# Adaptive-norm block with linear attention and a routed expert stage: padding rows written block by block during the attention stage, a later turn of the weight maxima, filling matmuls, one turning transfer per tile

## What is computed

```python
def reference(x, qkv_w, qkv_b, out_w, out_b, W_in, in_norm_w, Wr, expert_bias, Wg, Wu, Wd, enorm_w,
              out_norm_w, W_out, c, wmod):            # x: 16 x 256 x 128
    sa, ca, ga, sb, cb, gb = split(silu(c) @ wmod, 6)  # one row per batch; |ga|, |gb| at least 0.25
    h = layernorm(x) * (1 + ca) + sa
    x = x + ga * attention(h)
    h = layernorm(x) * (1 + cb) + sb
    return x + gb * experts(h)

def attention(h):                                      # 16 heads of 8
    q, k, v = heads(h @ qkv_w.T + qkv_b)
    q, k = relu(q) + 1e-6, relu(k) + 1e-6
    kv = cumsum(einsum('bhld,bhle->bhlde', k, v), axis=2)
    num = einsum('bhld,bhlde->bhle', q, kv)
    den = maximum(einsum('bhld,bhld->bhl', q, cumsum(k, axis=2)), 1e-6)
    return (num / den) @ out_w.T + out_b

def experts(s):                                        # 4096 tokens, 8 experts, 2 of them per token
    h = rmsnorm(s @ W_in.T) * in_norm_w
    logits = h @ Wr.T
    idx = top_k(logits + expert_bias, 2)
    gates = softmax(logits[idx])
    out = sum(gates[e] * rmsnorm((silu(h @ Wg[e].T) * (h @ Wu[e].T)) @ Wd[e].T) * enorm_w[e] for e in idx)
    return (rmsnorm(out) * out_norm_w) @ W_out.T
```

## Time and profile before

| | |
|---|---|
| median of 3 runs | 413.69 us (413.61 to 415.18) |
| the profiled execution | 414.08 us |
| its span | 412.2 us |
| mean granted TensorE clock | 0.939 |
| busy: TensorE, VectorE, ScalarE, GpSimd | 354.4, 323.8, 291.9, 236.5 us |

### The profile page before, as it was taken

One profiled execution on the slowest core, in us unless ns is written; L12 is line 12 of the kernel. 1 busy time (PEld: TensorE's weight loads), 2 busy tenths in 40 slices (PEclk: granted clock), 3 DMA queues, 4 the chain that ended last, 5 costly groups with the idle time before them and its releaser, 6 DMA issues.

```text
span 412.2 us, 12923 instructions
## 1 busy us (share of the span) xinstructions
PE 354.4 (86%) x3757; PEld 307.9 (75%) x3758; DVE 323.8 (79%) x1037; ACT 291.9 (71%) x814; POOL 236.5 (57%) x211
## 2 busy tenths in 40 slices
PE   7899998999999999982069999999999999990464
PEld 4788886888888888861049889989899898980443
DVE  5568998899999999976928887878778877870696
ACT  5465776888888888546328878778778787773595
POOL 0665585688888888856341645454454445453441
PEclk9999998999999999995559999999999999997698
DMA  7899000000000000111423333333333333213833
GB/s 217 356 368 363 2 28 26 8 30 27 26 26 26 26 26 26 34 40 51 131 40 54 68 71 70 62 71 60 64 64 71 60 69 65 57 34 110 351 94 94
DMA packets 46563, 35.68 MB, mean 87 GB/s; under 512 B 36291, under 2 KB 42070, under 8 KB 45750
## 3 DMA queue, kind: packets, MB, share of 16 engines
q1 hardware_dynamic: 41862, 25.40, 21.9%
q0 software_dynamic: 4544, 9.39, 7.0%
q10 hardware_dynamic: 128, 0.53, 0.5%
HBM read 18.69 MB, written 13.47 MB: 78 GB/s over the span
## 4 chain that ended last, share of the span: by engine, by line
PE 70%; DVE 10%; ACT 6%; issue 5%; DMA 4%; POOL 1%; SPq 1%; DVEq 0%; ACTq 0%; POOLq 0%
PE bank L1474 12%; PE bank L1723 9%; PE bank L1724 8%; PE bank L1725 8%; PE bank L1738 4%; PE bank L1740 4%; PE bank L1554 4%; PE bank L1739 4%; PE bank L1497 3%; DVE prod L960 2%; ACT junk L835 2%; DVE wmaxs L1056 1%; PE bank L1561 1%; DMA cst<-consts 1%; PE bank L1581 1%
## 5 line engine op out<-in xcount | busy, mean ns | idle before, releaser
L559 POOL DMA_INDIRECT expert_rows<-late,to_place x78 | 79.2, 1015 | 85.9 <-DVE late L1333 73.3
L1723 PE MATMUL bank<-late,w_hi 128*128 128x256 f16 x312 | 86.4, 277 | 15.1 <-DMA late<-dispatched 13.7
L1724 PE MATMUL bank<-late,w_hi 128*128 128x256 f16 x312 | 86.4, 277 | 0.0
L1725 PE MATMUL bank<-late,w_lo 128*128 128x256 f16 x312 | 86.3, 276 | 0.0
L518 POOL TENSOR_TENSOR kv<-kv,v 128x1024 f32<-128x1024 f32 x32 | 67.7, 2134 | 32.0 <-ACT kv L686 32.0
L1319 DVE SCALAR_TENSOR_TENSOR kv<-bank,uscale,kv 128x512 f32<-128x512 f32 x78 | 58.5, 750 | 30.4 <-ACT kv L777 18.6
L536 POOL DMA_INDIRECT dispatched<-rows,pos x64 | 67.3, 1051 | 25.7 <-issue 18.2
L1474 PE MATMUL bank<-cst,kv 128*128 128x128 f32 x576 | 74.3, 279 | 0.0
L777 ACT ACTIVATE kv<-bank,descale 128x512 f32<-128x512 f32 x78 | 53.6, 687 | 24.0 <-PE bank L1725 20.1
L1474 PEld LDWEIGHTS bank<-cst,kv 128*128 128x128 f32 x576 | 68.9, 193 | 0.3 <-issue 0.2
L783 ACT ACTIVATE kv<-kv 128x512 f16<-128x512 f32 x78 | 48.8, 625 | 16.8 <-DVE kv L1319 12.3
(11 more groups left out here) (233 smaller groups left out, 733.2 us busy)
## 6 DMA issues: line engine op xcount, KB each, us to landing
late<-wguT SPq DMA_DIRECT2D x1, 4096.0 KB, 17.8
late<-expert_rows SPq DMA_DIRECT2D x1, 2064.0 KB, 10.9
gates_bc<-gate_rows SPq DMA_DIRECT2D x1, 2048.0 KB, 6.9
wd<-wdT SPq DMA_DIRECT2D x1, 2048.0 KB, 25.0
out<-kv SPq DMA_DIRECT2D x16, 128.0 KB, 1.8
late<-dispatched SPq DMA_TRANSPOSE x78
expert_rows<-late,to_place POOLq DMA_INDIRECT x78
late<-expert_rows SPq DMA_DIRECT2D x1, 1032.0 KB, 6.5
```

The source lines that it names most:

```text
L559: pool.indirect_dma_start(ybuf, bass.IndirectOffsetOnAxis(ap=to_place[:, s, r:r + 1], axis=0), yt[:, s, r, :], None).then_inc(y_scat[s], 16)
L1723: mm(o, w_hi[:, w], hi, start=True, stop=False)
L1724: mm(o, w_hi[:, w], lo, start=False, stop=False)
L1725: last = mm(o, w_lo[:, w], hi, start=False, stop=True)
```

## The change

Seven edits:
1. `tail_f`, `tail`, `tail_done` and the eight late transfers go. In their place SP writes padding to all rows of all regions: block s (rows 256 s to 256 s + 255 of all eight regions, 17 blocks) goes out when the KV projection of batch s+2 is done and block s-2 has landed. `positions` of batch b waits for block b, so that real rows are written over padding. SP waits for the blocks and the scatters only after it has the table and its registers.
2. TensorE's turn of the weight maxima goes from the first half of step 7 to the second, `weight_power` behind the second products, the spreading matmul to the end of the step and into another bank, and `weight_scale` behind `positions` and `count_chosen`.
3. `norm_shift` computes both halves in one instruction.
4. `keep_busy`, matmuls of 512 columns whose results nobody reads, stands at six places: 5, 13, 3, 12, 24 and 8 of them. Ahead of the last 8, TensorE waits for the scatters.
5. One turning transfer of 256 columns per tile takes the place of two of 128.
6. The weight columns are addressed by bytes (`columns_of`).
7. ScalarE makes its four parts of `wd_hi` in a row, without the transfers between them.

```diff
+            regions = hbuf[0:E * REGION, :].rearrange("(e s p j) w -> s p e (j w)", e=E, p=16, j=R // 16)
+            padding = filler[0:E * R, :].rearrange("(e p j) w -> p e (j w)", p=16, j=R // 16)
+            for s in range(REGION // R):
+                sp.wait_ge(kv_ps, min(s + 3, B))
+                if s >= 2:
+                    sp.wait_ge(padded[s % 2], 16 * (s // 2))
+                sp.dma_start(regions[s], padding).then_inc(padded[s % 2], 16)
-            sp.wait_ge(tail_done, 1)
-            tail_regs = [sp.alloc_register(f"tail{e}") for e in range(E // 2)]
-            sp.load(tail_regs, tail[0:1, 0:E // 2])
-            for e in range(E // 2):
-                row = sp.snap(tail_regs[e], min_val=0, max_val=E * REGION - R)
-                sp.dma_start(hbuf[bass.ds(row, R), :].rearrange("(p j) w -> p (j w)", p=16),
-                             filler[e * R:(e + 1) * R, :].rearrange("(p j) w -> p (j w)", p=16)).then_inc(filled, 16)
-            sp.wait_ge(scattered[0], 16 * NT * K * (B // 2))
-            sp.wait_ge(scattered[1], 16 * NT * K * (B // 2))
-            sp.wait_ge(filled, 16 * (E + 1))
             sp.wait_ge(table_done, 1)
...
-                for half in range(2):
-                    sp.dma_start(hT3[:, s, half], hbuf16[bass.ds(row, R), half * D:(half + 1) * D],
-                                 transpose=True).then_inc(slot_ld[s], 16)
+                sp.dma_start(hT3[:, s], hbuf16[bass.ds(row, R), 0:2 * D], transpose=True).then_inc(slot_ld[s], 16)
...
                 sp.load(row_regs, tile_row[0:1, bass.ds(TURN * i, TURN)])
+                if not again_turn(i):
+                    sp.wait_ge(filled, 16)
+                    for s in range(2):
+                                sp.wait_ge(padded[s], 16 * ((REGION // R + 1 - s) // 2))
+                    sp.wait_ge(scattered[0], 16 * NT * K * (B // 2))
+                    sp.wait_ge(scattered[1], 16 * NT * K * (B // 2))
...
@@ norm_shift
-                for t in range(NT):
-                    last = nc.vector.tensor_scalar(nmr_[:, p, t:t + 1], mv_[:, p, t, 0:1], -1.0, rs_[:, p, t:t + 1],
-                                                   ALU.mult, ALU.mult)
-                last.then_inc(nm_done, 1)
+                nc.vector.scalar_tensor_tensor(nmr_[:, p, :], mv_[:, p, :, 0], -1.0, rs_[:, p, :], ALU.mult,
+                                               ALU.mult).then_inc(nm_done, 1)
@@ positions
                 dve.wait_ge(ohs_done, b + 1)
+                dve.wait_ge(padded[p], 16 * n)
@@ VectorE's step
                     running_products(att, 0)
-                    if scale:
-                        weight_power(att)
...
                 if att is not None:
+                    running_products(att, 1)
                     if scale:
-                        weight_scale(att)
-                    running_products(att, 1)
+                        weight_power(att)
...
                     positions(rb, rp, rn)
                     count_chosen(rb, rp)
+                if scale:
+                    weight_scale()
@@ running_state
-                    if scale and cc == 1:
-                        if t == 0:
-                            pe.wait_ge(wmax_done, 1)
-                            mm(MAX_ROW, wmax[:], ident, start=True, stop=True)
-                        else:
-                            pe.wait_ge(wpow_done, 1)
-                            mm(MAX_ALL, ones[0:1, :], wpow_row[:], start=True, stop=True)
+                    if scale and t and cc == 1:
+                        pe.wait_ge(wmax_done, 1)
+                        mm(MAX_ROW, wmax[:], ident, start=True, stop=True)
@@ TensorE's step
                     head_sums(att, 0)
                     head_sums(att, 1)
+                if scale:
+
+                    pe.wait_ge(wpow_done, 1)
+                    pe.wait_ge(ohs_done, rte[0] + 1)
+                    mm(MAX_ALL, ones[0:1, :], wpow_row[:], start=True, stop=True).then_inc(wall_ps, 1)
+
+            def keep_busy(bank, n):
+                for _ in range(n):
+                    mm(bank[:].rearrange("p (a n) -> p a n", n=P), ones16[:],
+                       ones16[:].unsqueeze(1).to_broadcast([P, 4, P]), start=True, stop=True)
@@ TensorE's drain
                 head_sums(b15, 1)
+                pe.wait_ge(cum_used[1][1], B)
+                keep_busy(CUM[1], 5)
                 spread(*b15)
                 ranks(*b13)
                 turn(*b14)
                 project(*b15)
                 into_experts(*b14)
+                keep_busy(CUM[1], 13)
                 ranks(*b14)
                 turn(*b15)
+                keep_busy(CUM[1], 3)
                 into_experts(*b15)
+                keep_busy(CUM[1], 12)
                 ranks(*b15)
...
             mm(TOTAL, ones16[:], oh_all[:, B, NT * K, :], start=True, stop=True).then_inc(total_ps, 1)
+            keep_busy(CUM[0], 24)
...
+            def columns_of(w, e, per_expert, at):
+
+                return w.bitcast(U8)[:, bass.ds(e * (2 * per_expert) + 2 * at, 2 * P)].bitcast(F16)
...
-                    w = bass.ds(e * F + (part * E * F + (h * (FC // 2) + c) * P), P)
+                    wh, wl = (columns_of(w[:], e, F, part * E * F + (h * (FC // 2) + c) * P) for w in (w_hi, w_lo))
...
             pe.wait_ge(moe_ld, 32)
+            pe.wait_ge(scattered[0], 16 * NT * K * (B // 2))
+            pe.wait_ge(scattered[1], 16 * NT * K * (B // 2))
+            keep_busy(CUM[0], 8)
             turn_of_tiles(0, first=True)
```

More of the change, by code:

```diff
@@ L21 @@
 U32 = mybir.dt.uint32
+U8 = mybir.dt.uint8
 ALU = mybir.AluOpType
@@ L315, in block_kernel @@
         ln_st, ln2_st = two("ln_st"), sem("ln2_st")
+        padded = two("padded")
         scattered, yb_ld, stored = two("scattered"), [sem(f"yb_ld{i}") for i in range(4)], four("stored")
@@ L320, in block_kernel @@
             sem(n) for n in ("count_done", "rank_ps", "ohs_done", "pos_done"))
-        ph2, total_ps, tail_done, table_done, wmaxs_done, wmax_done, wscale_done, whi_done, wlo_done = (
-            sem(n) for n in ("ph2", "total_ps", "tail_done", "table_done", "wmaxs_done", "wmax_done",
+        ph2, total_ps, table_done, wmaxs_done, wmax_done, wscale_done, whi_done, wlo_done = (
+            sem(n) for n in ("ph2", "total_ps", "table_done", "wmaxs_done", "wmax_done",
                              "wscale_done", "whi_done", "wlo_done"))
-        wpow_done = sem("wpow_done")
+        wpow_done, wall_ps = sem("wpow_done"), sem("wall_ps")
         gate_diff, gate_sig = sem("gate_diff"), sem("gate_sig")
@@ L342, in block_kernel @@
         MAX_ROW = CUM[1][0:1, THIRD * P:THIRD * P + P]
-        MAX_ALL = CUM[1][:, THIRD * P:THIRD * P + 1]
+        MAX_ALL = FFN[:, L + NT * E:L + NT * E + 1]
         SQUARE_STEPS = range(B - WN - DN // 2, B - WN)
@@ L755, in _ @@
             pipelined(act, step, drain)
[L757 to L769, removed]
+            for c in range(DN):
                 projection_high(c)
@@ L1072, in weight_power @@
             def weight_power(att):
-                dve.wait_ge(cum_ps[0][1], att[0] + 1)
+                dve.wait_ge(cum_ps[1][1], att[0] + 1)
                 then(nc.vector.tensor_reduce(wmax_row[:], MAX_ROW, AX.X, ALU.max))
@@ L1078, in weight_power, with weight_scale @@
                                         ALU.bitwise_and).then_inc(wpow_done, 1)
-            def weight_scale(att):
-                dve.wait_ge(cum_ps[1][1], att[0] + 1)
+            def weight_scale():
+                dve.wait_ge(wall_ps, 1)
                 then(nc.vector.tensor_copy(wpow[:], MAX_ALL))
@@ L1218, in second_shift @@
             def second_shift(b, p, n):
-                dve.wait_ge(ln2_rs, b + 1)
-                nc.vector.scalar_tensor_tensor(nmr2[:, p, :], mv2[:, p, :, 0], -1.0, rs2[:, p, :], ALU.mult,
-                                               ALU.mult).then_inc(ln2_nm, 1)
+                norm_shift(b, mv2, rs2, nmr2, ln2_rs, ln2_nm, p)
             def drain(b12, b13, b14, b15):
@@ L1262, in _ @@
             then(nc.vector.tensor_copy(total[:], TOTAL))
-            then(nc.vector.tensor_tensor(tail_f[:], total[0:1, :], cst[0:1, C_REG:C_REG + E], ALU.add))
-            nc.vector.tensor_copy(tail[:], tail_f[:]).then_inc(tail_done, 1)
             nj = TOK // R
@@ L1710, in experts @@
                 return [pe.snap(r, min_val=0, max_val=E - 1) for r in ex_regs]
+            def columns_of(w, e, per_expert, at):
+                return w.bitcast(U8)[:, bass.ds(e * (2 * per_expert) + 2 * at, 2 * P)].bitcast(F16)
             def gate_up(t, s, i, e, h, part):
                 if h == 0 and part == 0:
-                    pe.wait_ge(slot_ld[s], 32 * (i + 1))
+                    pe.wait_ge(slot_ld[s], 16 * (i + 1))
                 hi, lo = hT3[:, s, 0], hT3[:, s, 1]
@@ L1720, in gate_up @@
                     o = (G, U)[part][h][:, c * R:(c + 1) * R]
-                    w = bass.ds(e * F + (part * E * F + (h * (FC // 2) + c) * P), P)
```

(15 more changed lines are left out.)

2 lines of the change are left out of this document (removed).

## The result

The kernel after took 438.64 us at the median of 4 runs (431.51 to 444.23), the kernel before 414.44 beside it (4 runs). Two of the four ran in a disturbed state of the chip (444.2 us); the comparison leaves them out and gives a ratio of 1.042 [1.035, 1.050]. The forecast was 404.4, range 401.2 to 409.0: the change was forecast faster and is slower. The profiled execution took 433.13 us, span 431.3, against 414.08 and 412.2.

What follows compares the result with a forecast made beforehand. TensorE's work was taken as the bound almost everywhere except the hole at 185 to 210 us; 2.0 + 0.8 + 3.1 + 1.2 + 0.6 + 1.4 + 0.2 = 9.3 us won gave a median of 404.4, range 401.2 to 409.0.

Steps and rivals of the forecast that it cites:

- `norm_shift`: Two pairs a step on VectorE, each 0.16 us instead of 0.33; 0.8 us won in steps 3 to 6.
- the one of the other side: Rival: a padding block takes longer than a loop step, at 12 us a block about 433 us; chance 0.05.
- TensorE as the bound of the loop: In the loop TensorE's work sets the 10.3 us step, so savings on other engines there give next to nothing.
- Step 7: Loop step with the weight maxima: moving their turn and the scale later wins 2.0 us, bounds 0.5 and 2.4.
- Padding, what goes: Behind the last scatter: dropping the late padding transfers and loading SP's registers earlier wins 3.1 us.
- What comes: Seventeen padding blocks issued during the loop, 8.0 us each, landing before they are needed: cost 0.
- Filling and start of the expert stage: Fillers hold the clock in the drain, 1.2 us won, and half the clock loss in first sums, 1.4 us.
- the rival in which the 13 meet a lowered clock: Rival in the drain: the 13 fillers end 2.6 us late and the 1.2 is lost, 408.2 us; chance 0.1.
- The transfer that turns: Between SP's first issue and the expert stage's first matmul: one transfer saves 0.6 us, bounds 0 and 1.15.
- Addresses: Expert stage: weight addressing by bytes wins 0.2 us, bounds 0 and 1.3.

Runs made afterwards that it cites:

- 1: Kernel after with only `norm_shift` undone (two instructions again), beside a kernel before of 431.4 us: 423.05 us, ratio 0.980 to before.
- 2: Kernel before with only `norm_shift` put in one instruction, nothing else of the change: 454.62 us, ratio 1.049 to before.
- 3: Kernel after with one `norm_shift` instruction only for a step's first norm, two for the second: ratio 1.018 to before.
- 4: Kernel after with one `norm_shift` instruction only for a step's second norm, two for the first: ratio 0.987 to before.
- 5: Kernel after, `norm_shift` kept in one instruction, GpSimd's two products made to wait for the step's first `norm_shift`: 419.61 us, ratio 1.0095 to before.
- 9: The base: kernel after with `norm_shift` in two instructions, the same kernel as 1 run in another group: 410.84 us, ratio 0.991 to before.
- 10: The base with the weight maxima back in their old place: 410.73 us, ratio 0.989 to before.
- 7: The base without any filling matmuls (all `keep_busy` calls out): 413.70 us, ratio 0.9965 to before.
- 8: The base with two turning transfers of 128 columns per tile, as before: 414.19 us, ratio 0.997 to before.
- 11: The base with padding rows written as before, eight late transfers and no blocks in the loop: 412.85 us, ratio 0.993 to before.

## Why the prediction was wrong, step by step

- **`norm_shift`** is the step that failed. It priced the one instruction at 0.16 us from a row of the drain, where GpSimd only issues scatters, and said of the loop that "TensorE covers it". In the loop it stands up to 2.1 us behind a product, and a step takes 12.0 us and not 10.3. Forecast: 0.8 us won. Measured: 1.042 against 0.991 for the same kernel without it, 21 us lost. Experiments 1 to 5 show it. The rule cited above from the Trainium skill ("SBUF — State Buffer", Who interferes with whom) was at hand, and so was the row: the products in GpSimd's timeline. No rival had it; the one of the other side put the loss on the blocks.
- **TensorE as the bound of the loop** was too simple. GpSimd's products, four scatters and their gaps fill the 10.3 us too, with about 0.3 us of waiting, and VectorE, which gives it the positions, works 9.4 of 10 us. A delay of 2 us there has no cover.
- **Step 7**, 2.0 us: 0. The order of the maxima changes nothing that can be measured (9 and 10). What before lost there, 1.2 us, was the clock, which stayed up in the profiles of both 9 and 10; in 1, 7 and 8 it fell with the new order in place. What decides it is open.
- **Padding, what goes**, 3.1 us: right in its place, 2.6 in the hole (11 against 9). **What comes**, 0: false in the drain. "At the end the blocks are through" failed, because the last four all wait for the same step, and land in up to 13.7 us. The last scatter of batch 11 landed 4.5 us late. In the loop the blocks cost little: a step takes 10.36 us in the base and 10.31 in kernel 11. No `positions` waited for a block, as forecast.
- **Filling and start of the expert stage**, 1.2 + 1.4: 2.2 us together (7 against 9), by the profiled executions 2.0 in the first sums and 0.6 in the drain. In the drain they can also lose: the rival in which the 13 meet a lowered clock came true in after (3.98 us) and in 9.
- **The transfer that turns**, 0.6: 1.1 us in the hole; the ratios say 2.4 (8 against 9), part of it the 1.6 us of clock in the first sums.
- **Addresses**, 0.2: nothing to be seen; from the first `down` on all nine spans take 194.1 to 195.2 us. Not tried alone.

By the ratios the parts are 0 for step 7, 0.9 for padding, 2.2 for the fillers and 2.4 for the transfer, 5.5 us in all, and the base won 3.7. Each ratio is known to some 2 us, so the sum neither fits nor fails.

## What to carry to other kernels

Before one instruction takes the place of two on VectorE, count its inputs in SBUF and look at what GpSimd runs at that very time; a row of another stage does not price it. A form that saves 0.16 us made the step 1.7 us longer, since the delay went on into the engine that had blocked it. And background transfers cost little here until they met the small transfers on which a chain stands. Spreading them kept the scatters of the drain at 3.4 us and under (in the loop some took up to 6.7); that it shortens the whole is not shown.

## What was not expected of the hardware

- The blocked instruction waits for the GpSimd instruction in progress and no more: started at 117.94 it ended with the first product, though the second followed at once, and the two were as long as ever (4.22 us).
- Little decides at the start: 0.05 us behind a product's start (67.08 against 67.03 in the kernel after) the instruction took 2.09 us; 0.02 us behind one (119.88 in kernel 3) it took 0.14, and the two products 4.26 us and not 4.21. Where between the two it turns, no run shows.
- A scatter lands in 2.3 to 3.7 us without blocks beside it (kernel 11) and in up to 7.4 beside blocks of 1.06 MB in pieces of 8 KB.
